# Head-norm weights in the eviction of q and k, low halves later, x a slot ahead

## The reference

```python
xn  = ln(x) * (1 + sc1) + sh1                 # per image
q, k, v = split(xn @ w_qkv + b_qkv)           # 16 heads of 18
q, k = ln_head(q) * g_q, ln_head(k) * g_k     # block 0; block 1 has no head norm
q, k = ln_head(q) * g_q + b_q, ...            # block 2: weights and biases
o = softmax(q @ k.T / sqrt(18)) @ v
x = x + gate1 * (o @ w_proj + b_proj)
xn2 = ln(x) * (1 + sc2) + sh2
x = x + gate2 * (gelu(xn2 @ w1 + b1) @ w2 + b2)
```

## Time and profile before

| | |
|---|---|
| median of 3 runs | 4815.79 us (4815.25 to 4824.53) |
| profiled execution | 4821.86 us, its span 4820.1 |
| PE, PEld busy | 4250.8 us (88%), 3595.5 (75%) |
| DVE, ACT, POOL busy | 3660.6 us (76%), 2302.1 (48%), 1114.8 (23%) |
| instructions | 124616 |
| DMA | 141.59 MB, mean 29 GB/s |

### The profile page before, as it was taken

The page is one execution under the profiler, slowest core; times in us unless marked ns, Lnnn a source line. Parts: engine busy times, 40 slices in busy tenths (PEclk is TensorE's granted clock), DMA queues, the critical chain, the costliest instruction groups (busy, mean ns, idle before and its releaser), DMA issues. The chain is left out here.

```text
span 4820.1 us, 124616 instructions
## 1 busy us (share of the span) xinstructions
PE 4250.8 (88%) x46073; PEld 3595.5 (75%) x46073; DVE 3660.6 (76%) x7659; ACT 2302.1 (48%) x3894; POOL 1114.8 (23%) x2045
## 2 busy tenths in 40 slices
PE   6754899999999977999999999949989989898998
PEld 4543788888888865888888888737777777777776
DVE  5665889999888845777777777658778787877874
ACT  1212555555555534555555555435454444545443
POOL 1002222222222222222222222212222222222211
PEclk7576999999999988999999999979999999999998
DMA  3001111111111111111111111110010100001000
GB/s 76 21 0 52 32 29 29 29 29 29 29 29 29 27 54 30 30 29 29 29 29 29 29 29 29 37 43 24 20 30 20 28 21 28 21 20 30 20 26 18
DMA packets 122230, 141.59 MB, mean 29 GB/s; under 512 B 14446, under 2 KB 117780, under 8 KB 122112
## 3 DMA queue, kind: packets, MB, share of 16 engines
q1 hardware_dynamic: 121968, 139.75, 10.6%
q10 hardware_dynamic: 144, 0.22, 0.0%
HBM read 110.87 MB, written 29.06 MB: 29 GB/s over the span
## 5 line engine op out<-in xcount | busy, mean ns | idle before, releaser
L869 DVE TENSOR_REDUCE mx<-S 128x4 f32<-128x1024 f32 x768 | 902.7, 1217 | 190.3 <-PE S L1105 187.4
L627 ACT ACTIVATE pT<-S 128x1024 f32<-128x1024 f32 x768 | 745.3, 1023 | 363.2 <-PE S L1133 358.9
L575 ACT ACTIVATE hf<-M 128x512 f32<-128x512 f32 (+1 forms) x480 | 266.2, 555 | 841.8 <-DVE hl L860 597.1
L504 POOL TENSOR_SCALAR hh<-hf 128x512 fp32r<-128x512 f32 (+1 forms) x480 | 286.8, 602 | 1037.2 <-ACT hf L575 1016.4
L1133 PE MATMUL S<-qT,kT 32*128 32x256 f32 x9216 | 427.3, 296 | 65.6 <-ACT pT L627 62.8
L1146 PE MATMUL A<-pT,V 128*32 128x256 f32 x6144 | 416.0, 389 | 26.6 <-ACT pT L627 26.6
L1133 PEld LDWEIGHTS S<-qT,kT 32*128 32x128 f32 x9216 | 330.3, 186 | 138.8 <-ACT pT L627 90.3
L1185 PE MATMUL M<-xh,w_hi 128*128 128x256 f32 x1728 | 365.9, 293 | 3.5 <-POOL xh L480 3.5
L1224 PE MATMUL M<-w_lo,hh 128*128 128x288 f32 x1728 | 351.6, 304 | 0.0
L1185 PE MATMUL M<-xh,w_lo 128*128 128x256 f32 x1728 | 345.0, 281 | 0.0
L1185 PE MATMUL M<-xl,w_hi 128*128 128x256 f32 x1728 | 341.1, 281 | 0.2 <-DVE xm L792 0.2
(11 more groups left out here) (231 smaller groups left out, 9800.8 us busy)
## 6 DMA issues: line engine op xcount, KB each, us to landing
mid<-xbo SPq DMA_DIRECT2D x64, 288.0 KB, 3.2
xld<-mid SPq DMA_DIRECT2D x64, 288.0 KB, 3.0
xa<-mid SPq DMA_DIRECT2D x64, 288.0 KB, 3.6
gA<-gates SPq DMA_DIRECT2D x96, 144.0 KB, 3.3
gM<-gates SPq DMA_DIRECT2D x96, 144.0 KB, 3.0
xld<-in_x_dram SPq DMA_DIRECT2D x32, 288.0 KB, 3.5
xa<-in_x_dram SPq DMA_DIRECT2D x32, 288.0 KB, 3.5
out_dram<-xbo SPq DMA_DIRECT2D x32, 288.0 KB, 2.2
```

Source lines behind the costliest of these rows:

```text
L504: pool.tensor_scalar(hh[:, 2 * f:2 * f + m, :].rearrange("p m c -> p (m c)"), hf[:, f % 2, 0:m * T], 1.0, 0.0, ALU.mult, ALU.add).then_inc ...
L575: act.activation(hf[:, f % 2, 0:c], MBANK[f % 2][:, 0:c], ACT.Gelu if rot else ACT.Gelu_apprx_tanh).then_inc(s["m_hf"], 1)
L627: act.activation(pT[:, g % 2, 2 * h:2 * h + 2, :], S[:, 2 * h:2 * h + 2, :], ACT.Exp, scale=float(HD) ** -0.5).then_inc(s["a_ex"], 1)
L869: dve.tensor_reduce(mx[:, p, :, :], S[:, r:r + 2, :].rearrange("p a (t k) -> p a t k", t=NT), AX.X, ALU.max).then_inc(s["a_mx"], 1)
```

## The change

- The head-norm weights and biases leave DVE. They come as one small tensor with a value per partition (`cols`), and ACT applies them as scale and bias when it evicts the turned q and k, unrounded, into `turned`, which is the second half of `pT` (`A_turned`). It waits until the attention before has read that half, and the squares of the next image, which lie there too, wait for the low halves.
- POOL rounds `turned` to the high halves (`A_hi`, four instructions, behind `A_v`).
- The low halves are `turned` minus the high halves, both in SBUF. `A_lo(0)` comes after `A_max(5)`, `A_lo(1)` after the last `M_hl`, both ahead of `A_max(6)`. score(0) waits for the high halves alone, `A_scoresT(0)` for the low ones.
- The padding of `xn`, `xn2` and `on` is gone (two DVE instructions each). ACT evicts the chunk of 32 channels in three activations in place of one, straight to the places on the partitions where they are needed, and POOL no longer rounds `xm` and `xm2`; PE's waits count accordingly.
- SP loads x one slot ahead: the first x before the slots, and the next but one's in each slot ahead of the store. The last pass of the loop is written out for SP, as it loads nothing.

```diff
-gam = sb("gam", [P, 2 * HD])
-bet = sb("bet", [P, 2 * HD])
+cols = sb("cols", [P, 4])
...
+turned = flat[:, 2048:4096].rearrange("p (x q c) -> p x q c", x=2, q=QUADS)
...
-if nxt is not None:
-    load_x(nxt)
 if a is not None:
     load_gA(a)
     load_xa(a)
...
     load_m(sp, layer, range(V_RING, NCH))
+if nxt is not None and not (isinstance(nxt, int) and nxt + 1 == last):
+    load_x(nxt + 1)
 if d is not None:
     store(d)
...
+load_x(first)
+slots(sp, slot, peel=1)
 sp.wait_ge(s["m_out"], upto("m_out", last, 0))
...
-wait(pool, "a_xf", n, 3)
-constant_wait(pool)
-pool.tensor_scalar(xm[0:KP, :], xf[0:KP, FULL, :], 1.0, 0.0, ALU.mult, ALU.add).then_inc(s["a_xh"], 1)
...
+def A_hi(n, f):
+    for x, done, hi in ((qT, "a_qt", "a_qhi"), (kT, "a_kt", "a_khi")):
+        wait(pool, done, n, f + 1)
+        constant_wait(pool)
+        of = turned[:, 0 if done == "a_qt" else 1, 2 * f:2 * f + 2, :]
+        pool.tensor_scalar(x[:, 0, 2 * f:2 * f + 2, :], of, 1.0, 0.0, ALU.mult, ALU.add).then_inc(s[hi], 1)
...
 A_v(p)
+A_hi(p, 0)
+A_hi(p, 1)
...
+if c == FULL:
+    wait(act, "m_h", n, 0)
+for to, r in ([(xf2[:, c, :], slice(0, P))] if c < FULL else
+              [(xf2[TAIL, c, :], TAIL), (xm2[TAIL, :], TAIL), (xm2[0:REST, :], TAIL)]):
+    act.activation(to, MBANK[c // 2][r, (c % 2) * T:(c % 2 + 1) * T], ACT.Identity,
+                   bias=mmod[r, c:c + 1], scale=mmod[r, 3 + c:4 + c]).then_inc(s["m_xf"], 1)
...
+wait(act, "a_klo", n, 0)
...
-def A_hi(n, f):
-    wait(act, "a_T", n, 2 * f + 1)
-    act.activation(qT[:, 0, 2 * f:2 * f + 2, :].rearrange("p m c -> p (m c)"), S[:, 2 * f, :], ACT.Identity).then_inc(s["a_qhi"], 1)
-    wait(act, "a_T", n, 2 * f + 2)
-    act.activation(kT[:, 0, 2 * f:2 * f + 2, :].rearrange("p m c -> p (m c)"), S[:, 2 * f + 1, :], ACT.Identity).then_inc(s["a_khi"], 1)
+def A_turned(n, f):
+    if f == 0:
+        wait(act, "a_pv", n, 0)
+        if eps is not None:
+            wait(act, "a_hs", qk_run(n), 1)
+    for x, done in ((0, "a_qt"), (1, "a_kt")):
+        wait(act, "a_T", n, 2 * f + x + 1)
+        to = turned[:, x, 2 * f:2 * f + 2, :].rearrange("p m c -> p (m c)")
+        if rot:
+            op = act.activation(to, S[:, 2 * f + x, :], ACT.Identity, scale=cols[:, x:x + 1], bias=cols[:, 2 + x:3 + x])
+        elif eps is not None:
+            op = act.activation(to, S[:, 2 * f + x, :], ACT.Identity, scale=cols[:, x:x + 1])
+        else:
+            op = act.activation(to, S[:, 2 * f + x, :], ACT.Identity)
+        op.then_inc(s[done], 1)
 def A_shift(n):
...
-def A_heads_norm(n, m):
+def A_heads_norm(n):
     wait(dve, "a_T", n, 0)
     by_head = qk.rearrange("p t (x h d) -> p t x h d", x=2, d=HD)
     scale = ny[:, :].rearrange("p (t x h) -> p t x h", t=NT, x=2)
-    for x in range(2):
+    for x, slots_of in ((0, qs), (1, ks)):
         for j in range(NT):
-            to = ks[:, j, :, 0:HD] if x and not rot else by_head[:, j, x]
-            op = dve.tensor_tensor(to, by_head[:, j, x], scale[:, j, x].unsqueeze(2).broadcast_to([P, H, HD]), ALU.mult)
-    own(op)
-    if m is not None:
-        M_hl(m, 1)
-    if rot:
-        for j in range(NT):
-            part = qk[:, j, 0:2 * D].rearrange("p (x h d) -> p x h d", h=H, d=HD)
-            step = dve.tensor_tensor(part, part, gam[:, :].rearrange("p (x d) -> p x d", d=HD)
-                                     .unsqueeze(2).broadcast_to([P, 2, H, HD]), ALU.mult)
-        own(step)
-        if m is not None:
-            M_hl(m, 2)
-    for x, slots_of in ((0, qs), (1, ks))[0:2 if rot else 1]:
-        for j in range(NT):
-            step = dve.tensor_tensor(slots_of[:, j, :, 0:HD], by_head[:, j, x],
-                                     (bet if rot else gam)[:, x * HD:(x + 1) * HD].unsqueeze(1).broadcast_to([P, H, HD]),
-                                     ALU.add if rot else ALU.mult)
-    step.then_inc(s["a_nrm"], 1)
+            op = dve.tensor_tensor(slots_of[:, j, :, 0:HD], by_head[:, j, x],
+                                   scale[:, j, x].unsqueeze(2).broadcast_to([P, H, HD]), ALU.mult)
+    op.then_inc(s["a_nrm"], 1)
 def A_lo(n, f):
-    for x, (bank, done, hi) in enumerate(((S[:, 2 * f, :], "a_qlo", "a_qhi"), (S[:, 2 * f + 1, :], "a_klo", "a_khi"))):
+    for x, (to, done, hi) in enumerate(((qT, "a_qlo", "a_qhi"), (kT, "a_klo", "a_khi"))):
         wait(dve, hi, n, f + 1)
-        t = (qT, kT)[x]
-        dve.tensor_tensor(t[:, 1, 2 * f:2 * f + 2, :].rearrange("p m c -> p (m c)"), bank,
-                          t[:, 0, 2 * f:2 * f + 2, :].rearrange("p m c -> p (m c)").bitcast(F32), ALU.subtract).then_inc(s[done], 1)
+        dve.tensor_tensor(to[:, 1, 2 * f:2 * f + 2, :], turned[:, x, 2 * f:2 * f + 2, :],
+                          to[:, 0, 2 * f:2 * f + 2, :].bitcast(F32), ALU.subtract).then_inc(s[done], 1)
...
 if p is not None:
-    A_lo(p, 0)
-    A_lo(p, 1)
     A_max(p, 0)
     A_max(p, 1)
...
 if p is not None:
     A_max(p, 4)
     A_max(p, 5)
+    A_lo(p, 0)
 if m is not None:
     M_hl(m, 3)
     M_hl(m, 4)
+if p is not None:
+    A_lo(p, 1)
 if p is not None:
     A_max(p, 6)
     A_max(p, 7)
...
 if g == 0:
-    wait(pe, "a_qlo", n, 2)
-    wait(pe, "a_klo", n, 2)
+    wait(pe, "a_qhi", n, 2)
+    wait(pe, "a_khi", n, 2)
...
     wait(pe, "r_x3", n - first - 2, 0)
+wait(pe, "a_qlo", n, 2)
 wait(pe, "a_klo", n, 2)
```

More of the change, by code:

```diff
@@ L34 @@
 MIX = 3 * REST + 2
-WIDE = D + 2 * REST
+TAIL = slice(KP - REST, KP)
 FM = F // P
@@ L110, in build @@
         xa = sb("xa", [P, NT, D])
-        xn = sb("xn", [P, NT, WIDE])
+        xn = sb("xn", [P, NT, D])
         gA = sb("gA", [P, D])
@@ L155, in build @@
         xbo = sb("xbo", [P, 2, NT, D])
-        xn2 = sb("xn2", [P, NT, WIDE])
+        xn2 = sb("xn2", [P, NT, D])
         xb = xbo[:, 0, :, :]
@@ L325, in wait_normed, with slots @@
                     wait(eng, "a_nrm", qk_run(n), 1)
-            def slots(eng, slot):
+            def slots(eng, slot, peel=0):
                 slot(None, None, None, None, first)
@@ L333, in slots @@
                 slot(first + 2, first + 1, first, first + 3, first + 4)
-                with eng.Fori(start, last - 2) as n:
+                with eng.Fori(start, last - 2 - peel) as n:
+                    slot(n, n - 1, n - 2, n + 1, n + 2)
+                for n in range(last - 2 - peel, last - 2):
                     slot(n, n - 1, n - 2, n + 1, n + 2)
@@ L409, in _ @@
                     load_m(sp, layer, range(V_RING))
-                    slots(sp, slot)
+                    load_x(first)
+                    slots(sp, slot, peel=1)
                     sp.wait_ge(s["m_out"], upto("m_out", last, 0))
@@ L469, in A_xh @@
                         pool.tensor_scalar(xh[:, :, :], xf[:, 0:FULL, :], 1.0, 0.0, ALU.mult, ALU.add).then_inc(s["a_xh"], 1)
-                        wait(pool, "a_xf", n, 3)
-                        constant_wait(pool)
-                        pool.tensor_scalar(xm[0:KP, :], xf[0:KP, FULL, :], 1.0, 0.0, ALU.mult, ALU.add).then_inc(s["a_xh"], 1)
                     def M_xh(n):
                         wait(pool, "m_h", n, 0)
-                        for c in range(KC):
+                        for c in range(FULL):
                             wait(pool, "m_xf", n, c + 1)
                             constant_wait(pool)
-                            to, of = (xm2[0:KP, :], xf2[0:KP, c, :]) if c == FULL else (xh2[:, c, :], xf2[:, c, :])
-                            pool.tensor_scalar(to, of, 1.0, 0.0, ALU.mult, ALU.add).then_inc(s["m_xh"], 1)
+                            pool.tensor_scalar(xh2[:, c, :], xf2[:, c, :], 1.0, 0.0, ALU.mult, ALU.add).then_inc(s["m_xh"], 1)
                     def A_v(n):
@@ L563, in A_xf @@
                             wait(act, "a_xT", n, c // 2 + 1)
-                        r = KP if c == FULL else P
-                        act.activation(xf[0:r, c, :], MBANK[0 if rot else 1][0:r, (c % 2) * T:(c % 2 + 1) * T], ACT.Identity,
-                                       bias=amod[0:r, c:c + 1], scale=amod[0:r, 3 + c:4 + c]).then_inc(s["a_xf"], 1)
+                        if c == FULL:
+                            wait(act, "a_qkv", n, 0)
+                        for to, r in ([(xf[:, c, :], slice(0, P))] if c < FULL else
+                                      [(xf[TAIL, c, :], TAIL), (xm[TAIL, :], TAIL), (xm[0:REST, :], TAIL)]):
+                            act.activation(to, MBANK[0 if rot else 1][r, (c % 2) * T:(c % 2 + 1) * T], ACT.Identity,
+                                           bias=amod[r, c:c + 1], scale=amod[r, 3 + c:4 + c]).then_inc(s["a_xf"], 1)
                     def M_gelu(n, f):
@@ L633, in A_ohi @@
                         wait(act, "a_nT", n, 2)
-                        act.activation(om[0:KP, :], ABANK[1][0:KP, 0:T], ACT.Identity).then_inc(s["a_oh"], 1)
+                        for rows in (TAIL, slice(0, REST)):
+                            act.activation(om[rows, :], ABANK[1][TAIL, 0:T], ACT.Identity).then_inc(s["a_oh"], 1)
                     def R_x(n, part, nxt):
```

(32 more changed lines are left out.)

46 lines of the change are left out of this document (16 added, 30 removed).

## The result

The changed kernel takes 4872.16 us (median of 4 runs, 4870.35 to 4880.51) against 4818.83 for the kernel before (4 runs): ratio 1.0113, 95% interval 1.0095 to 1.013. It is slower by 53 us where 15 were forecast, and above the end of the range (4866). The profiled execution took 4880.51 us, its span is 4878.8, 58.7 more than before.

A forecast was written before the change was run, and what follows sets the result against it. Layers 0 and 1: PE bounds each slot's first half, DVE its second; layer 2's first half waits on DVE, late for x's DMA. 115.9 − 97.7 + 3.7 − 6.9 = +15.0 on 4815.8 gave 4831 us, range 4792 to 4866.

The forecast's parts named there:

- Low halves moved: Layers 0 and 1, second half of the slot on DVE: +1.87 us per slot, 62 slots, +115.9; free in layer 2.
- Layer 2, −3.62 in 27 slots: Earlier x and weights off DVE end PE's wait before turning q and k, and its half clock: −97.7 us.
- More evictions for chunk 2: Two more ScalarE activations before the exponentials, hidden by 0.88 us of idle: cost 0, at most 0.25 per slot.
- R3: Rival: the GpSimd hop or the longer ScalarE eviction is late by 0.25 us in 91 slots; 4854 us, chance 0.06.
- The clock: Layers 0 and 1: PE's new gap of 1.71 us before turning nm costs no clock speed, no loss counted.
- R2: Rival: half the clock behind PE's new gap in every second slot of layers 0 and 1; +23, 4854 us, chance 0.10.
- Fills: First slots of a layer, no attention covering the preparation: low halves leave the path, 3 × −2.3 = −6.9 us.
- The hop over GpSimd: score(0) waits for ScalarE's eviction, then GpSimd's rounding: cost 0, with 0.7 us in hand.

The follow-up runs named there:

- e2: Changed kernel with the chunk of 32 channels evicted by one ScalarE activation and the two rounded copies made by GpSimd; 4847.38 us.
- e8: Changed kernel with the last two low halves done twice in their late place, the second result unused; 5053.91 us.
- e1: Changed kernel with all four low halves back ahead of the first reduction; 4864.98 us.
- e5: Kernel before, with x loaded a slot ahead as the only change; 4720.61 us, ratio 0.9799.
- e4: Changed kernel with the load of x back in its old place, behind the store; 4874.99 us.
- e10: Changed kernel with nine unused products added on PE in layers 0 and 1, ahead of the turn of nm; 4853.91 us.
- e7: As e1, but in layer 1 alone the low halves take one input from PSUM and score(0) waits for them; 4838.65 us.

## Why the prediction was wrong

The direction and the two large terms were right. The sum was small beside them, and two terms set at nothing were not nothing.

- *Low halves moved, +1.87 a slot.* Right: with the wait of e2 gone, slots are 42.18, 1.88 over 40.30. No run moves the low halves and nothing else, but e8 bears the term out: DVE's chain ends the second half. The wording that went with it was incomplete: it is not the place alone. In the form that the change gives them, the early place costs too (e1, 41.85 and 47.99). What costs is the pair: both inputs in SBUF, and a rounding on GpSimd just ahead.
- *Layer 2, −3.62 in 27 slots.* Right: 46.09 expected, 46.07 in e5 and 46.01 in e2, where chunk 2 costs nothing; the 46.42 of the changed kernel holds the next term. That either part alone removes the wait is shown by e4 and e5; so the weights on ScalarE bought nothing that the load didn't.
- *"More evictions for chunk 2", 0 with 0.25 as the upper bound.* Failed. By e2 it cost 0.30 a slot in layers 0 and 1 (42.48 − 42.18, 58 × 0.30 = 17 us) and 0.40 in layer 2 (46.41 − 46.01); from the first to the last nm of layer 2, e2 is 10 us shorter than the changed kernel. The three activations take 1.59 where one took 0.56, 1.03 more, and they start 0.03 behind the exponentials before them, where the one had overlapped those by 0.11. That is 1.17 to hide behind a cover of 0.88, 0.29 too much. R3 named the longer eviction, with 0.25 a slot and a chance of 0.06 that it shared with the hop.
- *The clock, "I count no loss".* Failed: 11 slots of 1.52 more, 17 us, and 2.1 in the second interval of layers 0 and 1 each (e10), 21 together. R2 had the mechanism, with 0.10, and half its price, read from layer 2 (0.73); that other waits there cover a part of it is argued, not shown. e10 and e8 show that the gap causes it. The Trainium skill, "TensorE: Matmul & The Clock Gate", section "HAM oscillation — how this bites in real kernels", names longer gaps only; the trace disagrees again, with a granted clock of 0.74 and 0.76 behind 1.76.
- *Fills, −6.9.* Outside the stretches of nm −11.6, but the first two intervals of layers 0 and 1 are 13.3 longer where the sum had 4 × 1.87 = 7.5. Of those 5.8 too much, 4.1 are the clock's. That the whole comes out 1.1 from the forecast is luck.
- *The hop over GpSimd, 0.* Right in the late placement, with 0.37 in hand in place of 0.7; where score(0) needs the low halves, as in layer 1 of e7, the hop is not free (0.40).

So 15.0 forecast, 17 for chunk 2 and 21 for the clock in layers 0 and 1, 9 that layer 2 fell short (−85.2 where −97.7 + 3.7 was forecast; chunk 2 again, by e2), and −5 outside the stretches of nm (−11.6 where −6.9 was forecast) make 57 of the 58.7 of the profile; what is left is not taken apart. Either miss alone would have stayed inside the range; R2 and the second half of R3 came together, and the chances had no share for that.

What the trace before held and the prediction passed over: `xl<-hf,xh`, also a VectorE subtraction of 128x512 with both inputs in SBUF, beside copies of V on GpSimd. The records of its twin, which mostly runs while GpSimd is idle, and its own (min, median and max in ns):

```profile
L791 DVE TENSOR_TENSOR xl<-xf,xh x96: 677/692/1175, 419.4 to 4657.2; 128x512 fp32r<-128x512 f32 x96
L791 DVE TENSOR_TENSOR xl<-hf,xh x96: 691/1246/1248, 522.2 to 4784.5; 128x512 fp32r<-128x512 f32 x96
```

These are 0.69 against 1.25 in the median for the same shape. In the whole trace 91 of these 192 records are longer than 0.9 us, each of them overlaps a copy of V on GpSimd, and none of the others does. That was a sign that such an instruction is held up by GpSimd, and that a late place for the low halves had a reason.

Open: why the clock falls behind the gap of 1.76 in some slots and not in others with the same gap. It does not look like chance: within a layer the long slots of e4 stand eight apart, those of e2 ten. What sets that distance no run here shows.

## What to carry to other kernels

Work taken from an engine pays only in the stretch where that engine ends last: here 292 us of VectorE's work went, and the one DMA moved ahead made the gain, 95 us when it was the only change. Where a sum is the difference of two large terms, every edit set at nothing needs its cover measured against all that it adds, start to end, and a new idle gap on PE needs the price of a slower clock behind it. Before the source of an operand is moved from PSUM to SBUF, look at what GpSimd does at that moment.

## What the runs showed of the hardware that was not expected

- A VectorE subtraction of 128x512 with two SBUF inputs and a GpSimd rounding of 128x512 go in step when they run at the same time (e1): 1.09 and 1.05 us, one of each per 1.01, against 0.69 and 0.62 apart; with one input in PSUM, 0.68 and 0.62 side by side (e7).
- PE at half its clock (1.2 GHz) behind idle gaps of 1.76 us in 11 of 58 steady slots (7 and 5 in e4 and e2) and of 2.96 in 57 of 58 (e8); with nine products put into the gap, in none (e10).
- Three ScalarE activations of 32x256 take 1.59 us, 0.53 each; one of 96x256 took 0.56.
